# A graph layer with a 17-tap convolution on one core: a weight sum by an adding transfer, sub-convolutions in parts, and slots shared by two engines, in the first group

## The reference, cut to what matters

```python
h = jnp.maximum(_layernorm(x, axis=-1), 0.0)
# the layer, on h:
c = relu(_bn(_conv1d(hT, conv1_w, 0)))          # over features
c = _bn(_conv1d(c, conv2_w, 8))                 # 17 taps over the nodes
x_conv = transpose(relu(c + hT))
s = h @ w_se.T + b_se                           # 3 numbers for each node
sq = sum(s * s, -1)
A = exp(-(sq[:, :, None] + sq[:, None, :] - 2 * s @ s.T)) * mask
msg = relu(h @ w_msg.T + b_msg)
x_nmp = A @ msg
# a gated recurrent cell on [x_conv, x_nmp] with state h
out = x + (1 - z) * tanh(gi_n + r * gh_n) + z * h
```

## Time and profile before

| | us |
|---|---|
| median of 3 runs | 287.91 (287.84 to 287.97) |
| the profiled execution | 288.4 |
| its span, first to last instruction | 286.5 |
| PE busy | 276.6 (97%) |
| DVE busy | 243.0 (85%) |
| ACT busy | 164.5 (57%) |
| POOL busy | 62.5 (22%) |

### The profile page before, as it was taken

One profiled execution on the slowest core, in us unless ns is written; L12 is line 12 of the kernel. 1 busy time (PEld: TensorE's weight loads), 2 busy tenths in 40 slices (PEclk: granted clock), 3 DMA queues, 4 the chain that ended last, 5 costly groups with the idle time before them and its releaser, 6 DMA issues.

```text
span 286.5 us, 5279 instructions
## 1 busy us (share of the span) xinstructions
PE 276.6 (97%) x1866; PEld 249.3 (87%) x1866; DVE 243.0 (85%) x551; ACT 164.5 (57%) x271; POOL 62.5 (22%) x124
## 2 busy tenths in 40 slices
PE   7899899999999999999999999999999999999993
PEld 6598886999888998899889998899988998899993
DVE  5998988978998889968998789969998787976565
ACT  3786468745565277545665267564674366561363
POOL 6500020831116102430026102340026100250000
PEclk9999999999999999999999999999999999999999
DMA  7600044566252512654153532645021540023002
GB/s 236 251 3 0 0 150 146 151 182 184 75 174 72 128 70 74 222 68 155 42 176 86 86 130 74 220 47 176 2 84 65 76 146 3 0 37 39 0 2 73
DMA packets 9373, 27.99 MB, mean 98 GB/s; under 512 B 2706, under 2 KB 3220, under 8 KB 8468
## 3 DMA queue, kind: packets, MB, share of 16 engines
q1 hardware_dynamic: 7184, 23.98, 24.0%
q0 software_dynamic: 2016, 3.67, 9.5%
q10 hardware_dynamic: 148, 0.01, 0.0%
HBM read 23.41 MB, written 7.91 MB: 109 GB/s over the span
## 4 chain that ended last, share of the span: by engine, by line
PE 67%; DVE 17%; issue 6%; ACT 5%; POOL 2%; DMA 1%; SPq 0%; DVEq 0%; ACTq 0%; POOLq 0%
PE ps L1194 20%; PE ps L1196 19%; PE ps L1195 19%; PE ps L1278 4%; PE ps L1244 3%; DVE stats L754 2%; DVE wt_lo L796 2%; DMA xin<-x_first 1%; ACT wt_hi L455 1%; POOL rstd L378 1%; PE ps L1255 1%; DVE aff L952 1%; DVE v_lo L877 1%; DVE y L897 1%; PE ps L1268 1%
## 5 line engine op out<-in xcount | busy, mean ns | idle before, releaser
L1194 PE MATMUL ps<-v_hi,wt_hi 128*128 128x256 f32 x320 | 92.6, 289 | 2.6 <-DVE v_lo L865 1.4
L1196 PE MATMUL ps<-v_hi,wt_lo 128*128 128x256 f32 x320 | 90.1, 282 | 0.0
L1195 PE MATMUL ps<-v_lo,wt_hi 128*128 128x256 f32 x320 | 89.9, 281 | 0.0
L1194 PEld LDWEIGHTS ps<-v_hi,wt_hi 128*128 128x128 f32 x320 | 60.3, 188 | 4.7 <-DVE wt_lo L796 1.8
L1195 PEld LDWEIGHTS ps<-v_lo,wt_hi 128*128 128x128 f32 x320 | 60.3, 188 | 0.3
L1196 PEld LDWEIGHTS ps<-v_hi,wt_lo 128*128 128x128 f32 x320 | 60.2, 188 | 0.0
L384 POOL TENSOR_TENSOR scale<-vpe,neg_half 128x8 f32<-128x8 f32 x6 | 10.6, 1768 | 87.8 <-DVE scale L771 87.8
L1194 PE MATMUL ps<-h_hi,wt_hi 128*128 128x512 f32 (+1 forms) x67 | 26.2, 391 | 0.2 <-ACT gate L612 0.2
L1196 PE MATMUL ps<-h_hi,wt_lo 128*128 128x512 f32 (+1 forms) x67 | 25.8, 386 | 0.0
L1195 PE MATMUL ps<-h_lo,wt_hi 128*128 128x512 f32 (+1 forms) x67 | 25.7, 383 | 0.0
L607 ACT ACTIVATE gate<-ps,par 128x512 f32<-128x512 f32 x14 | 9.6, 687 | 20.6 <-PE ps L1196 20.6
(11 more groups left out here) (160 smaller groups left out, 621.5 us busy)
## 6 DMA issues: line engine op xcount, KB each, us to landing
w<-ln_rows SPq DMA_DIRECT2D x6, 1024.0 KB, 4.7
mask<-adj_t SPq DMA_DIRECT2D x8, 512.0 KB, 3.5
out<-x_t SPq DMA_DIRECT2D x7, 512.0 KB, 5.1
out<-gate POOLq DMA_DIRECT2D x14, 256.0 KB, 4.1
xin<-x_nm SPq DMA_DIRECT2D x6, 512.0 KB, 3.3
xt<-x_t SPq DMA_DIRECT2D x6, 512.0 KB, 5.7
w<-w_conv SPq DMA_DIRECT2D x1, 576.0 KB, 5.9
gate<-w_gate SPq DMA_DIRECT2D x1, 576.0 KB, 6.9
```

Source lines behind the costliest of these rows:

```text
L1194: pe.matmul(dst, wt_hi[:, blk, :], hi, start=start, stop=False)
L1195: pe.matmul(dst, wt_hi[:, blk, :], lo, start=False, stop=False)
L1196: return pe.matmul(dst, wt_lo[:, blk, :], hi, start=False, stop=stop)
```

## The change

It touches group 0 alone.

- **A sum of weights by transfers.** `sums_of_four(1)` on DVE is gone. SP loads taps 1 of each four straight into `fab[:, :, 1, :]` (256 KB in 512 pieces of 512 bytes), behind `wg` and ahead of `bias` and `mask`. POOL waits for that (`pair_landed`) and then starts a transfer that adds taps 3 onto it (`pair_summed`), right behind L418. ACT's `lot_high(8)` waits for `pair_summed`.
- **Sub-convolutions in parts.** `sub_conv_first` issues, for all taps, first high weights by high data, then high weights by low data, then low weights by high data, and waits ahead of each part only for what that part reads. The number of products is the same.
- **Slots by two engines.** `distances(dve, 0)` is gone. ACT makes the high parts and the copies (five instructions in three steps), DVE the low parts and the squares (four instructions, then one). Factor -0.5 goes into the squaring.

```diff
@@ block.sync
             sp.dma_start(wg, w_gate).then_inc(wg_landed, 16)
+            sp.dma_start(fab[:, :, 1, :], pairs[:, :, 1, :]).then_inc(pair_landed, 16)
             sp.dma_start(bias[:], bias_in).then_inc(bias_landed, 16)
@@ block.gpsimd
             pool.tensor_tensor(row[32:33, :], row_raw[32:33, :], row_hi[32:33, :], ALU.subtract).then_inc(row_split, 1)
+            pool.wait_ge(pair_landed, 16)
+            pool.dma_start(fab[:, :, 1, :], pairs[:, :, 3, :], accum_op=ALU.add).then_inc(pair_summed, 16)
             pool.wait_ge(row_split, 3)
@@ block.scalar
                 elif n == 8:
-                    act.wait_ge(sums_ready, 5)
+                    act.wait_ge(pair_summed, 16)
@@ messages(g, first), between the copies to s_sb and those to msg
+                if g == 0:
+                    slots_first(0)
+            def slots_first(step):
+                ...
+                if step == 0:
+                    act.wait_ge(s_ready, 2)
+                    act.wait_ge(pool_set, 5)
+                    act.activation(hi, s_sb[:, :, 0:3].unsqueeze(2).broadcast_to([P, GB, 2, 3]),
+                                   ACT.Copy).then_inc(slot_hi, 1)
+                elif step == 1:
+                    act.wait_ge(slot_hi, 1)
+                    act.activation(halves[:, :, :, 0, :], hi.bitcast(F32), ACT.Copy)
+                    act.wait_ge(slot_sq, 3)
+                    act.activation(left[:, :, 12], sq[:], ACT.Copy).then_inc(slot_hi, 1)
+                    act.wait_ge(slot_lo, 1)
+                    act.activation(halves[:, :, :, 1, :], lo.bitcast(F32), ACT.Copy)
+                else:
+                    act.wait_ge(slot_lo, 2)
+                    act.activation(right[:, :, 14:16], left[:, :, 12:14].bitcast(F32), ACT.Copy).then_inc(slots_ready, 1)
@@ ACT's order
             messages(0, 3)
+            slots_first(1)
             m_shared(0, 1)
+            slots_first(2)
             lot_high(11)
@@ block.vector
+            def slots_low_first(step):
+                ...
+                if step == 0:
+                    dve.wait_ge(s_ready, 2)
+                    dve.scalar_tensor_tensor(out=ssq[:], in0=s, scalar=-0.5, in1=s, op0=ALU.mult,
+                                             op1=ALU.mult).then_inc(slot_sq, 1)
+                    dve.wait_ge(slot_hi, 1)
+                    dve.tensor_tensor(left[:, :, 6:12]..., s..., left[:, :, 0:6]..., ALU.subtract).then_inc(slot_lo, 1)
+                    dve.wait_ge(slot_sq, 1)
+                    dve.tensor_tensor(sq[:], ssq[:, :, 0], ssq[:, :, 1], ALU.add).then_inc(slot_sq, 1)
+                    dve.wait_ge(slot_sq, 2)
+                    dve.tensor_tensor(sq[:], sq[:], ssq[:, :, 2], ALU.add).then_inc(slot_sq, 1)
+                    return
+                dve.wait_ge(slot_hi, 2)
+                dve.tensor_tensor(left[:, :, 13], sq[:], left[:, :, 12], ALU.subtract).then_inc(slot_lo, 1)
@@ DVE's order
             lot_low(4)
-            sums_of_four(1)
             level1(0)
@@
             join_b(0, 1)
+            slots_low_first(0)
             lot_low(7)
+            slots_low_first(1)
             v_low_u(0, 2)
             lot_low(8)
-            distances(dve, 0)
             lot_low(9)
@@ block.tensor
+            def sub_conv_first(q):
+                i, v = q // 3, q % 3
+                dst = quarter(v)
+                taps = SUBS[q]
+                pe.wait_ge(wt_hi_ready, LOT_OF_SUB[q])
+                if i == 0:
+                    pe.wait_ge(v_hib_ready, 1 + min(v, 1))
+                    if v == 0:
+                        pe.wait_ge(c_ready, 1)
+                else:
+                    pe.wait_ge(v_hiu_ready, 3 if i == 2 else 1 + min(v, 1))
+                    if v == 0:
+                        pe.wait_ge(mbs_ready, i)
+                    elif i == 1:
+                        pe.wait_ge(mb_ready, v)
+                    else:
+                        pe.wait_ge(y_ready, 2 + v)
+                for k, blk in enumerate(taps):
+                    pe.matmul(dst, wt_hi[:, blk, :], v_hi[:, q, k:k + QUART, :], start=k == 0, stop=False)
+                if i == 0:
+                    pe.wait_ge(v_lob_ready, 1 + min(v, 1))
+                else:
+                    pe.wait_ge(v_lou_ready, 3 if i == 2 else 1 + min(v, 1))
+                for k, blk in enumerate(taps):
+                    pe.matmul(dst, wt_hi[:, blk, :], v_lo[:, q, k:k + QUART, :], start=False, stop=False)
+                pe.wait_ge(wt_lo_ready, LOT_OF_SUB[q])
+                for k, blk in enumerate(taps):
+                    last = pe.matmul(dst, wt_lo[:, blk, :], v_hi[:, q, k:k + QUART, :], start=False,
+                                     stop=k == len(taps) - 1)
+                last.then_inc(conv2_ps, 1)
@@ PE's order: nine times
-            sub_conv(0, q)
+            sub_conv_first(q)
```

More of the change, by code:

```diff
@@ L148, in gnn_kernel @@
         out_stored = [sem(f"out_stored{c}") for c in range(NCH)]
+        pair_landed, pair_summed = sem("pair_landed"), sem("pair_summed")
         out_filled = sem("out_filled")
@@ L179, in gnn_kernel @@
             sem("rows_ready"))
+        slot_hi, slot_lo, slot_sq = sem("slot_hi"), sem("slot_lo"), sem("slot_sq")
         dist_ps, e_ready, a_ready, nmp_ps, n_hi_ready, n_lo_ready = (
@@ L260, in distances @@
             s = s_sb[:, :, 0:3]
-            base = 10 * g
+            base = 10 * (g - 1)
             engine.tensor_copy(six(left, 0), twice(s)).then_inc(s_steps, 1)
@@ L569, in raw_messages @@
                 act.activation(msg[:, 0:8, :], msg[:, 0:8, :], ACT.Relu).then_inc(msg_ready, 2)
+            def slots_first(step):
+                left, right = slots[:, 0], slots[:, 1]
+                halves = right[:, :, 0:12].rearrange("p b (r h k) -> p b r h k", r=2, h=2)
+                hi = left[:, :, 0:6].rearrange("p b (r k) -> p b r k", k=3)
+                lo = left[:, :, 6:12].rearrange("p b (r k) -> p b r k", k=3)
+                if step == 0:
[13 more added lines that the diff above has]
+                    act.activation(right[:, :, 14:16], left[:, :, 12:14].bitcast(F32), ACT.Copy).then_inc(slots_ready, 1)
             def factor_rows(g):
@@ L968, in reset @@
                 dve.tensor_tensor(gn[c][:], bank(5), gn[c][:], ALU.add).then_inc(v_ready, 1)
+            def slots_low_first(step):
+                left = slots[:, 0]
+                s = s_sb[:, :, 0:3]
+                if step == 0:
[3 more added lines that the diff above has]
+                    dve.wait_ge(slot_hi, 1)
+                    dve.tensor_tensor(left[:, :, 6:12].rearrange("p b (r k) -> p b r k", k=3),
+                                      s.unsqueeze(2).broadcast_to([P, GB, 2, 3]),
+                                      left[:, :, 0:6].rearrange("p b (r k) -> p b r k", k=3),
+                                      ALU.subtract).then_inc(slot_lo, 1)
+                    dve.wait_ge(slot_sq, 1)
[5 more added lines that the diff above has]
+                dve.tensor_tensor(left[:, :, 13], sq[:], left[:, :, 12], ALU.subtract).then_inc(slot_lo, 1)
             def update(g, c):
@@ L1053, in _ @@
             raw = w2[:, 0:16, :].rearrange("p (k r) c -> p r k c", r=4)
-            def sums_of_four(r):
-                dve.tensor_tensor(fabk[:, r], raw[:, r], raw[:, r + 2], ALU.add).then_inc(sums_ready, 1)
-            sums_of_four(0)
+            dve.tensor_tensor(fabk[:, 0], raw[:, 0], raw[:, 2], ALU.add).then_inc(sums_ready, 1)
             lot_low(2)
@@ L1279, in gather @@
                 last.then_inc(nmp_ps, 1)
+            def sub_conv_first(q):
[28 more added lines that the diff above has]
+                last.then_inc(conv2_ps, 1)
             def sub_conv(g, q):
                 i, v = q // 3, q % 3
-                if g == 0:
-                    pe.wait_ge(wt_lo_ready, LOT_OF_SUB[q])
                 if i == 0:
-                    if v == 0 and g == 0:
-                        pe.wait_ge(c_ready, 1)
-                    elif v == 0 and g <= BY_MATMUL:
+                    if v == 0 and g <= BY_MATMUL:
                         pe.wait_ge(msg_ready, 2 * g + 2)
@@ L1401, in _ @@
             keep_busy(5)
-            sub_conv(0, 0)
-            sub_conv(0, 1)
-            sub_conv(0, 2)
+            sub_conv_first(0)
+            sub_conv_first(1)
+            sub_conv_first(2)
             pe.wait_ge(row_split, 3)
@@ L1407, in _ @@
             messages(0, 3)
-            sub_conv(0, 3)
-            sub_conv(0, 4)
-            sub_conv(0, 5)
+            sub_conv_first(3)
+            sub_conv_first(4)
+            sub_conv_first(5)
             factor_transposes(0)
-            sub_conv(0, 6)
+            sub_conv_first(6)
             distance(0)
-            sub_conv(0, 7)
-            sub_conv(0, 8)
+            sub_conv_first(7)
+            sub_conv_first(8)
             gather(0, 0, 5)
```

1 line of the change is left out of this document (added).

## The result

| | before | after |
|---|---|---|
| median | 287.91 (287.84 to 288.01, 5 runs) | 286.30 (286.18 to 286.37, 5 runs) |
| the profiled execution | 288.4 | 286.3 |
| its span | 286.5 | 284.4 |
| granted clock of TensorE in it | 1.00 | 1.00 |

The ratio is 0.9942, 95% interval 0.9931 to 0.9953: 1.61 us faster, against a forecast of 286.2 and a gain of 1.76.

The account below looks back on a forecast made before the run. DVE's join releasing sub-convolution 7 in group 0 was taken as the bound, PE just not late. DVE's 0.60 + 1.72 - 0.48 - 0.08 = 1.76 takes the median from 287.91 to 286.15, said as 286.2; range 285.5 to 287.3.

Parts of the forecast that it names:

- sub-convolution 7's wait: PE in group 0: its wait for `y`, 0.76, ends last, 0.15 behind DVE's first join; start moves from 31.37 to 29.61.
- DVE's chain: DVE in group 0: 0.60 + 1.72 - 0.48 - 0.08 = 1.76 less, between 1.6 and 1.8; join ends at 29.46.
- DVE's gap: DVE's wait for ACT's `v_hi`: stays about 0.71 as ACT moves with DVE, so the 0.60 is kept whole.
- The wait for ACT's squares: DVE's second slot step, `slots_low_first(1)`: squares done 0.17 after 24.7 to 24.9, DVE arrives at 24.96; nothing, or 0.1.
- PE's chain: PE to the end of `distance` in group 0: 30.61 - 0.6 - 0.15 - 0.46 = 29.4, near 29.2 if hand-overs shrink.
- the 0.46 for the slots' wait: PE ahead of the transposes at 28.17: the wait of 0.46 goes, as the slots are complete near 25.4.
- sub-convolution 4's wait: PE in group 0: a wait estimated at 0.15, the length of a hand-over, goes.
- ACT: Five small copies of about 0.1 to 0.25 each, delaying `mbs` by 0.5 at most; costed at nothing.
- The transfers: Weight sum ready between 15.5 (cost by bytes) and 26.0 (by pieces), taken as 17 to 18; wanted at 20.57, hidden.
- (a): Rival: PE or ACT is late instead, gain 1.3 or 1.0, time 286.6 to 286.9; chance 0.20.
- (b): Rival: adding transfer late, each us after 20.6 costs one; 289.5 half way, 291.5 by pieces; chance 0.09.
- (c): Rival: later groups wait for something fixed in time and absorb the gain, 287.8; chance 0.04.

Follow-up runs that it names:

- The kernel with the transfer a little late: Changed kernel with POOL's adding transfer started only when PE's sub-convolution 0 is done; 287.68, 1.38 over the changed kernel.
- the two others with 11: Kernel before with only the sub-convolutions of group 0 in parts, 287.95; kernel before with only the weight sum by two transfers, 287.38.
- the kernel with the transfer started at u: Changed kernel with POOL's adding transfer started only when DVE's differences u are there; 289.77, 3.47 over the changed kernel.

## Why the prediction was right, and where it was not

**What bounds the kernel, right, with one wait overlooked.** The time follows DVE's join in every run in which PE had time to spare: 0.55 for 0.60 less on DVE, 1.02 for 1.1 less, and nothing for an earlier PE. But the prediction calls sub-convolution 7's wait the one that ends last, and it is not the last that hangs on this join. PE waits once more in group 0, for ACT's gate; before, then after:

```profile
44.30 0.50 PE L1194 MATMUL ps<-h_hi,wt_hi 128*128 128x512 f32 x1 [0.17 <-ACT gate L612]
...
42.20 0.50 PE L1243 MATMUL ps<-h_hi,wt_hi 128*128 128x512 f32 x1 [0.16 <-ACT gate L643]
```

Followed back in the changed kernel, it goes over ACT's normalised x (39.92) to a small instruction of DVE (`nmr`, 39.72 to 39.88), to POOL's `rstd` (37.66) and to DVE's chain behind the join. It moves with the join, so the sum was not touched. It is why an earlier join still paid where PE was already the late one at sub-convolution 7.

**DVE's chain, right to 0.08.** The sum was 1.76, the trace has 1.68 and the medians 1.61. The two slot steps cost 0.64 in all, not 0.56: 0.02 in the first place, 0.06 in the second. That DVE's gap would stay came true. The wait for ACT's squares was within the forecast's "nothing, or 0.1", and may not have been nothing: ACT made them at 24.34 to 24.56, DVE came 0.64 after the lot's start, at 24.58, where 0.60 is the usual step. Up to 0.04 of the 0.06 can be this wait; the profile shows no idle time there.

**PE's chain, a term mis-sized.** I had put PE at the end of `distance` at 29.2 to 29.4, which is 28.8 to 29.0 with the offset; it was there at 28.17 + 0.44 = 28.61. And without the parts I had it at 30.0, 29.57 with the offset, and concluded that the parts decide by 0.4. PE was at 29.26 without them. The step that failed is the 0.46 for the slots' wait. An idle time is counted from the modelled end of the last product, 0.28 after its start, but the next product can start 0.12 after it. The last product ahead of the transposes, before and in the change without the parts:

```profile
27.43 0.28 PE L1196 MATMUL ps<-v_hi,wt_lo 128*128 128x256 f32 x1
...
26.74 0.28 PE L1245 MATMUL ps<-v_hi,wt_lo 128*128 128x256 f32 x1
```

Without the wait the transposes came 0.12 behind it (26.86), and 0.74 behind it before (28.17): 0.62 was to be had, not 0.46. The other term, sub-convolution 4's wait, was put at 0.15 and gave 0.25: with the offset taken off, the last product moved from 26.99 to 26.74. The two make up 0.26 of the 0.3. The consequence was a wrong value for one part of the change: it moves PE and not the time. The sum was not touched, since I had taken DVE as the later.

**ACT, right.** Its small copies took 0.22 to 0.25 each and overlapped: the three between `msg` and `mbs` delayed `mbs` by 0.37 (24.20 to 24.57). But for the 0.04 above nothing waited for them.

**The transfers, right, nearer to the cheap bound than I took.** By pieces or by bytes was the open question. A packet of 512 bytes cost 5 x 16 x 0.422 / 521 = 0.065 us where one of 2 KB, in the adding store, costs 0.234, 3.6 times as much: it goes nearly by bytes. POOL's issue went up from 0.89 to 1.52, the landing from 4.1 to 4.7. The forecast was a sum at 17 to 18 with 3 us to spare; it was 16.4 with 3.7. The plain transfer landed at 11.4, as taken; POOL started 0.3 behind that. The Trainium skill's rule that GpSimd shares its SBUF interfaces with VectorE, with contention where VectorE has two SBUF inputs (GPSIMD Engine Reference, Specifications), did not bear on the time, as the issue was hidden; the issue took 1.52 in each of the eight runs that have it. POOL's start 0.6 us after its release in the two runs with the late transfer may come from this rule, and no run here tells it from another cause. The estimate of 2.6 us by the Trainium skill (DMA: Bandwidth & Descriptors, Anatomy of one DMA — SWDGE (gpsimd) path) is less than the 4.7 measured; the measurement decides.

**The rivals.** (a), that PE is late, did not hold: 0.63 of idle time, against 0.2 to 0.4. Its price was too high as well: with no parts at all the gain was 1.68, where it has 1.3. (b), the slower one, was right in its mechanism and its price: each us beyond the slack costs a us (3.47 for 3.35, 1.38 for 1.34). It needed 3.7 us more of delay to begin, and another 1.6 to end slower than before. (c), that something absorbs the gain, did not hold.

**The size of the gain.** 1.61 instead of 1.76 is 0.08 of DVE and 0.07 that the runs' scatter of 0.2 does not allow to settle.

## What to carry to other kernels

A wait on the busiest engine is worth no more than what the *next* late thing leaves of it. Look for the chain whose end releases the last wait of a stage, count its instructions, and cut there; then look for later waits that hang on the same chain. Feeding TensorE earlier was worth nothing while VectorE's join came later; where the two were level, it was worth 0.3. A gap on the late engine is room for any work of its own whose inputs are ready: moving one instruction into a gap of 0.71 us gave 0.65 us. A transfer can take an addition off the late engine if it has slack; measure the slack by delaying it, as here nothing was taken up beyond it.

## What was not expected of the hardware

- The idle time that the profile shows ahead of a pipelined product is less than what its removal gives: 0.46 shown, 0.62 gained, as products start 0.12 apart while each is shown 0.28 long.
- POOL started its transfer about 0.6 us after its release (18.17 to 18.84, and 15.6 to 16.18), in both runs where a wait for another engine stood before it; behind the wait for the plain transfer alone it was some 0.3 (11.4 to 11.72). Both late starts lie 0.05 to 0.06 behind the end of an instruction of DVE (18.09 + 0.69 = 18.78, 15.42 + 0.71 = 16.13), but in the changed kernel POOL started at 11.72 in the middle of one (11.45 to 12.14). The cause is open.
- The kernel with the transfer a little late scattered by 0.60 us over 11 runs, against 0.23 and 0.28 for the two others with 11. That its chain runs through the landing of a transfer does not explain it by itself: the kernel with the transfer started at u has such a chain too and scattered by 0.26 over 5 runs. The cause is open.
